# adaLN block on one core: weight-search counts by matmul, row maxima split before the transpose, and two moved products

## What is computed

```python
mod = (silu(c) @ wmod).reshape(8, 6, 1, 128)      # sa, ca, ga, sb, cb, gb
h = layernorm(x) * (1 + ca) + sa
x = x + ga * attention(h)                         # 16 heads of 8 dims, ALiBi bias, causal softmax
h = layernorm(x) * (1 + cb) + sb
x = x + gb * ffn(h)

def perturb(w):                                   # for W1, W2, b1, b2
    a = abs(w); s = sort(a.ravel()); k = int(n * 0.1 / 2)
    tier = where(a >= s[n - k], -1, where(a <= s[k - 1], 1, 0))
    return w + 0.8 * w * tier

def ffn(x):
    probs = softmax((layernorm(x) * gamma + beta) @ Wr + br)
    # expert 0 has the clean weights; experts 1 to 7 share the perturbed ones
    return sum_e probs[e] * (gelu(x @ W1[e] + b1[e]) @ W2[e] + b2[e])
```

## Time and profile before

| | |
|---|---|
| Time, median of 3 runs | 303.92 us (300.79 to 307.02) |
| Profiled execution: its own time | 301.41 us |
| Profiled execution: span, first to last instruction | 299.6 us |
| Mean granted PE clock | 0.901 |
| Busy: PE, DVE, ACT, POOL | 222.9, 213.6, 150.9, 135.8 us |
| Instructions | 5332 |

### The profile page before, as it was taken

The page is one execution under the profiler, slowest core; times in us unless marked ns, Lnnn a source line. Parts: engine busy times, 40 slices in busy tenths (PEclk is TensorE's granted clock), DMA queues, the critical chain, the costliest instruction groups (busy, mean ns, idle before and its releaser), DMA issues.

```text
span 299.6 us, 5332 instructions
## 1 busy us (share of the span) xinstructions
PE 222.9 (74%) x1799; PEld 150.0 (50%) x1799; DVE 213.6 (71%) x681; ACT 150.9 (50%) x337; POOL 135.8 (45%) x220
## 2 busy tenths in 40 slices
PE   2750575719886888877868488785983999999994
PEld 2340453517564666555546255453351467676674
DVE  2663499926998987989989359989586378626275
ACT  2322134326887757976786357763541743434430
POOL 8430089923855616536354024344635644443240
PEclk9999997556999979999999559997796699999999
DMA  7845556350250530433506200000000000101011
GB/s 218 178 94 139 150 141 244 86 144 0 73 142 21 150 82 23 128 85 82 150 0 170 63 1 2 3 2 2 2 1 2 0 1 2 35 1 37 0 35 35
DMA packets 17551, 20.42 MB, mean 68 GB/s; under 512 B 1446, under 2 KB 15413, under 8 KB 16317
## 3 DMA queue, kind: packets, MB, share of 16 engines
q1 hardware_dynamic: 14964, 18.98, 23.7%
q10 hardware_dynamic: 2048, 0.98, 1.2%
q0 software_dynamic: 512, 0.13, 0.3%
HBM read 14.70 MB, written 5.26 MB: 67 GB/s over the span
## 4 chain that ended last, share of the span: by engine, by line
PE 41%; DVE 25%; DMA 15%; POOL 10%; issue 6%; ACT 2%; SPq 0%; ACTq 0%; DVEq 0%; POOLq 0%
PE bank L746 10%; PE bank L728 10%; DMA Qs<-nmT 8%; DVE msk L939 7%; DVE nmax L970 5%; POOL hid L387 4%; PE bank L653 3%; DMA Ks<-parts 3%; DMA parts<-part 3%; PE bank L632 2%; PE bank L808 2%; PE bank L610 2%; DVE nmax L966 2%; PE bank L627 1%; POOL PT L400 1%
## 5 line engine op out<-in xcount | busy, mean ns | idle before, releaser
L400 POOL TENSOR_SCALAR_AFFINE_SELECT PT<-PT 128x256 f32<-128x256 f32 (+1 forms) x96 | 47.6, 500 | 80.1 <-ACT PT L453 77.4
L453 ACT ACTIVATE PT<-bank 128x512 f32<-128x512 f32 x96 | 53.5, 586 | 14.8 <-PE bank L627 13.7
L970 DVE TENSOR_REDUCE nmax<-bank 128x2 f32<-128x512 f32 x64 | 43.7, 683 | 20.7 <-PE bank L610 20.5
L365 POOL TENSOR_TENSOR ex<-eul,lg 128x32 f32<-128x32 f32 x4 | 21.7, 5428 | 27.8 <-DVE lg L1030 27.8
L606 PE MATMUL bank<-mask 128*128 128x256 bf16 x64 | 19.8, 309 | 12.0 <-DVE nmax L970 11.5
L610 PE MATMUL bank<-Ks,Qs 78*128 78x256 bf16 x128 | 28.6, 309 | 0.0
L966 DVE TENSOR_REDUCE nmax<-bank 128x4 f32<-128x512 f32 x32 | 21.7, 677 | 9.6 <-PE bank L603 9.6
L632 PE MATMUL bank<-Qs,Ks 80*128 80x256 bf16 x128 | 26.8, 293 | 0.6 <-ACT PT L453 0.5
L653 PE MATMUL bank<-PT,Vx 128*32 128x256 f32 x256 | 22.3, 422 | 5.4 <-POOL PT L400 5.2
L460 ACT ACTIVATE msk<-w1a,cand 128x512 bf16<-128x512 f32 x31 | 22.2, 715 | 6.7 <-DVE cand L933 3.9
L939 DVE TENSOR_SCALAR_CACHE_REDUCE msk<-w1a,cand 128x512 bf16<-128x512 f32 x31 | 23.1, 746 | 1.1
(11 more groups left out here) (181 smaller groups left out, 520.7 us busy)
## 6 DMA issues: line engine op xcount, KB each, us to landing
Qs<-parts SPq DMA_DIRECT2D x8, 576.0 KB
Ks<-parts SPq DMA_DIRECT2D x8, 576.0 KB
parts<-part SPq DMA_DIRECT2D x8, 384.0 KB, 2.9
rows_bc<-rows_out SPq DMA_DIRECT2D x4, 512.0 KB, 6.6
parts<-part SPq DMA_DIRECT2D x8, 128.0 KB, 3.6
out<-ob SPq DMA_DIRECT2D x3, 256.0 KB, 2.3
x_all<-in_x ACTq DMA_DIRECT2D x5, 128.0 KB, 8.5
w_sb<-in_w SPq DMA_DIRECT2D x2, 256.0 KB, 5.2
```

The lines of the kernel that those rows point to most:

```text
L400: gp.affine_select(out=v, in_=v, compare_op=ALU.is_ge, fill=0.0, base=0, pattern=[[0, v.shape[1]], [1, P]], channel_multiplier=-1).then_in ...
L453: act.activation(PT[:, e % 2, j], psE[u % 2][:, :], ACT.Exp).then_inc(q["exp_done"], 1)
L970: ve.tensor_reduce(nmax[:, b % 2, 1, h:h + 2], bank.rearrange("p (h k) -> p h k", h=2), axis=AX.X, op=ALU.max, negate=True).then_inc(q["ma ...
```

## The change

It does seven things.

- **Counts.** DVE's compares no longer accumulate; they write 0/1 masks. PE adds them with eight matmuls of one column each (counts), DVE copies the two sums to acc (count_copy), and total adds over partitions as before. counts stands right behind s_unit(t, 0), ahead of both e_units.
- **ACT's order.** exp_unit 0 and 1 stand ahead of the two sign passes, which are apart now; the U copy and exp_unit 2 stand behind them.
- **PE's order.** s_unit 1 ahead of pv, total behind pv, then s_unit 2, e_unit 2, ut, and OT and Y at the end of the step, in psX, the bank that the search uses (claim_x makes the next user wait for the last reader).
- **Maxima.** They are split by query in SBUF by DVE (split_maxima), and transposed as bf16 high and low parts in one product; ACT copies both at once.
- **Attention's front.** It begins one step earlier (t = -10), and ACT and DVE take up its products a step after PE makes them.
- **Fixed rows.** The constant rows of Qs and Ks come a rotation at a time, one with each stack; b1, b2 and x of batches 3 to 7 are loaded behind the first stack, and the magnitudes of W1 and W2 are taken later.
- **b2.** Its sizes, masks and perturbation move from steps -3 and -2 to steps 0 and 1; b1's rank masks start two steps later.

The core of the diff (`psO`, `psU` and `psX` are PSUM banks 4, 5 and 7):

```diff
 # SP
+            def fixed_rows(r):
+                sp.dma_start(Qs[R_PROD:R_S, r].rearrange("r h t -> r (h t)"), q_const).then_inc(const_in[r], 16)
+                sp.dma_start(Ks[R_PROD:R_E, r].rearrange("r h t -> r (h t)"), k_const).then_inc(const_in[r], 16)
-            sp.dma_start(Qs[R_PROD:R_S], rot(q_const)).then_inc(q["const_in"], 16)
-            sp.dma_start(Ks[R_PROD:R_E], rot(k_const)).then_inc(q["const_in"], 16)
                     stack(b)
+                    if b + 1 < ROTS:
+                        fixed_rows(b + 1)
+                    if b == 0:
...
+                        for k in range(3, B):
+                            sp.dma_start(x_all[:, k], x[k].rearrange("(i p) d -> p i d", p=P)).then_inc(x_in[k], 16)
 # ACT
             for t in range(T_FIRST, T_END):
-                if sel_bit(t) is not None:
-                    sign_counts(t)
...
                 exp_unit(t, 0)
+                exp_unit(t, 1)
+                if n is not None:
+                    sign_count(n, 2, w1a)
                 b = batch_at(t, AT_NMT)
...
+                    act.activation(nmT[:, b % 2, :], psO[0:3 * NH, 0:S], ACT.Copy).then_inc(q["nmr_done"], 1)
+                if n is not None:
+                    sign_count(n, 3, w2a)
...
+                b, g, e = lagged(t, E_LAG + 1)
+                if b is not None:
...
+                    act.activation(U[:, e % 2], psO[:, 0:S], ACT.Copy).then_inc(q["u_done"], 1)
+                exp_unit(t, 2)
 # PE
+            def counts(n):
+                claim_x((q["cnt_copied"], n + 1))
+                pe.wait_ge(q["m_dve"], n + 1)
+                for col in range(2):
+                    for j in range(NC):
+                        last = mm(psX[:, col:col + 1], msk[:, col, j * P:(j + 1) * P], ones_b[:, 0:1],
+                                  start=(j == 0), stop=(j == NC - 1), skip_group_check=True)
+                last.then_inc(q["cnt_done"], 1)
...
             for t in range(T_FIRST, T_END):
                 s_unit(t, 0)
+                counts(n)
...
                 e_unit(t, 0)
                 e_unit(t, 1)
+                s_unit(t, 1)
                 pv(t)
+                total(n)
+                s_unit(t, 2)
+                e_unit(t, 2)
+                ut(t)
                 b = batch_at(t, AT_OT)
...
                 b = batch_at(t, AT_Y)
                 if b is not None:
+                    claim_x((q["x2_done"], b + 1))
                     pe.wait_ge(q["wog_done"], b + 1)
...
-                    pe.wait_ge(q["a_done"], min(t - E_LAG - 1, B * G))
                     for i in range(NBLK):
+                        last = mm(psX[:, i * P:(i + 1) * P], AT[:, i * P:(i + 1) * P], woTg[:, b, :], start=True, stop=True)
 # DVE
-                    last = ve.tensor_scalar(msk[:, col], w[:, :], cand[:, col:col + 1].bitcast(F32), 0.0, op0=ALU.is_lt,
-                                            op1=ALU.add, accum_out=acc[:, col:col + 1])
+                    last = ve.tensor_scalar(msk[:, col], w[:, :], cand[:, col:col + 1].bitcast(F32), None, op0=ALU.is_lt)
+            def count_copy(n):
+                v.wait_ge(q["cnt_done"], n + 1)
...
+                ve.tensor_copy(acc[:, 0:2], psX[:, 0:2]).then_inc(q["cnt_copied"], 1)
+            def split_maxima(b):
...
+                ve.tensor_copy(nmHL[:, k, :, 0:NH], nmax[:, k]).then_inc(q["nm_self"], 1)
+                v.wait_ge(q["nm_self"], b + 1)
+                ve.tensor_tensor(nmHL[:, k, :, 2 * NH:3 * NH], nmax[:, k], nmHL[:, k, :, 0:NH], op=ALU.subtract).then_inc(q["nm_split"], 1)
```

More of the change, by code:

```diff
@@ L761, in _ @@
                 s_unit(t, 0)
+                counts(n)
+                b = batch_at(t, AT_NMT)
+                if b is not None:
+                    pe.wait_ge(q["nm_split"], b + 1)
+                    if b == 0:
+                        pe.wait_ge(q["dve_set"], SETS["all"])
+                    if t > E_LAG + 1:
+                        pe.wait_ge(q["u_done"], min(t - E_LAG - 1, B * G))
+                    for i in range(NBLK):
+                        last = mm(psO[0:3 * NH, i * P:(i + 1) * P], nmHL[:, b % 2, i, :], mask5[:, HG, :], start=True, stop=True)
+                    last.then_inc(q["nmT_done"], 1)
@@ L778, in _ @@
                     last.then_inc(q["y_done"], 1)
-                s_unit(t, 1)
-                e_unit(t, 2)
-                total(n)
-                b = batch_at(t, AT_NMT)
-                if b is not None:
-                    pe.wait_ge(q["max_done"], 3 * G * (b + 1))
-                    if b == 0:
-                        pe.wait_ge(q["dve_set"], SETS["all"])
-                    if t > E_LAG:
-                        pe.wait_ge(q["u_done"], min(t - E_LAG, B * G))
-                    for i in range(NBLK):
-                        last = tr(psO[0:NH, i * P:(i + 1) * P], nmax[:, b % 2, i, :], ident[:, :])
-                    last.then_inc(q["nmT_done"], 1)
@@ L1119, in _ @@
                 maxima(t, 0)
[L1120 to L1124 removed]
+                if n is not None:
+                    count_copy(n)
+                maxima(t, 1)
+                if n is not None:
+                    decide(n)
+                    next_cand(n)
+                if t == -1:
+                    first_cand()
+                if sel_bit(t + 1) is not None:
+                    dve_counts(t + 1)
+                    if n is not None:
+                        after_next(n)
                 b = batch_at(t, AT_SPLIT)
@@ L1165, in _ @@
                                      op=ALU.mult).then_inc(q["a_done"], 1)
+                b = batch_at(t, AT_Y)
+                if b is not None:
+                    v.wait_ge(q["y_done"], b + 1)
+                    ve.tensor_tensor(x_all[:, b], x_all[:, b], psX[:, 0:S].rearrange("p (i d) -> p i d", i=NBLK),
+                                     op=ALU.add).then_inc(q["x2_done"], 1)
                 if t in LN1_AT:
```

157 lines of the change are left out of this document (70 added, 87 removed).

## The result

The changed kernel takes 329.37 us (median of 4 executions, 327.95 to 329.72), the kernel before beside it 304.05 (300.79 to 307.02): ratio 1.0865, 95% interval 1.0808 to 1.0922. It is slower by 8.7%, 23 us above the forecast and 9 above its range. (The ratios in this document are formed from each kernel's undisturbed executions alone, those near its fastest, the medians from all, and the kernel before runs from 297 to 308 us; so ratios and medians can differ by one to three per cent.)

A forecast was written before the change was run, and what follows sets the result against it. Bounds: transfers first, then DVE, search rounds of 5.18 us (4.1 DVE's work), lastly PE in the FFN. Terms -4.2, -2.5, +8.5, +3, -1 gave +3.8 on 301.4: 305.2, plus 1, 306 us; range 291 to 320.

The forecast's parts named there:

- the search rounds with exponentials: Decision 6 to 30: a closed loop through four engines makes the 24 rounds 132.7 us against 124.2, +8.5 us.
- the clock: Search rounds: two more rounds with PE at 1.2 GHz, +3 us; as rival, half the rounds, 322 us, chance 0.18.
- The loop: Plain search round: decision, masks, counts, scores, exponentials, sign passes and total in series, 4.87 us.
- The long round: Search round from r = 3 to r = 0: maxima product and copy add 0.5 us, OT and V 0.45.
- The wait for Y's sum: Search, once a batch: next step's counts wait for DVE's sum of Y into x, 3.07 instead of 1.65, so 1.4 us.
- Start: Before the first scores: the parts' second write takes about 3.6 us instead of 7.8, -4.2 us.
- Steps 0 to 6: First scores to decision 6: cheaper masks, b2's work added on DVE, maxima rows landing just in time, -2.5 us.
- Steps 31 to 40: After the search rounds: OT and Y at other places, the FFN's front the same, -1 us.
- the loop would have to be 0.5 us a round shorter for a gain of 2%: Search rounds, rival: loop shorter than added and start gains more, 292 us, chance 0.25; this was the argument against it.
- The port: Rival, DVE's masks: POOL's work holds them up 0.3 us a round, +9, 314 us, chance 0.10.
- The transfer at step 26: Search rounds: the wait of about 6 us for maxima rows was assumed gone; if it stayed, some 5 us more.
- What would make me wrong: Search rounds: ACT's sign passes start before that round's masks are counted; rounds of 3.7 us, kernel under 285 us.

The follow-up runs named there:

- e1: Changed kernel with both of ACT's sign passes put back ahead of exponentials 0 and 1: 299.44 us against 303.22 for the kernel before, ratio 0.976.
- e10: Changed kernel with ACT's copy of the maxima product ahead of both sign passes and PE's product behind both blocks of scores for the exponentials: 317.52 us, ratio 1.0512.
- e3: Changed kernel with six useless matmuls per step, in steps 6 to 30, ahead of total's wait for the sign passes: 322.07 us, ratio 1.0692.
- e7: e1 with PE's product of the maxima moved behind e_unit(t, 1): 290.48 us against 304.54 for the kernel before, ratio 0.9762.
- e8: e7 with total also put ahead of pv on PE: 288.80 us, ratio 0.9686 to the kernel before.
- e5: Changed kernel with DVE's accumulating compares back, no count matmuls or count copy, exponentials still first: 320.86 us against 304.54 for the kernel before, ratio 1.0796.
- e11: Kernel before with only the first two exponentials put ahead of the sign passes on ACT: 310.34 us against 301.60, ratio 1.031.

## Why the prediction was wrong

The mechanism was right and its size was not. The step that failed is **the search rounds with exponentials: +8.5 us**, together with **the clock: +3 us**: they measured +29.4. The forecast of the 24 rounds was 135.7 us, and they took 153.6. Within it two terms were mis-sized, the half microsecond for the maxima's product and copy, and the clock's.

- **The loop.** I added 4.87 us for a plain round; at 2.4 GHz it took 5.00, with every link within 0.2 of where I had put it. r = 1 to 2 was forecast at 5.49 (4.87 and QK's 0.6) and took 5.48, r = 0 to 1 at 6.27 (4.87 and 1.4) and took 6.30. e1 shows that the loop is the cause: opened at ACT, it gives 30 us back.
- **The long round.** I put 0.5 us on r = 0's product and copy of the maxima, and with the 0.45 of OT and V 5.8 for the round from r = 3 to r = 0; it took 6.83 (at a clock of 0.94) to 8.38, mean 7.80. I had costed the copy as a piece between two sign passes, and not the product that waits for DVE's split in front of the scores, nor that PV, and with it the total, stands behind a copy which waits for a whole sign pass. e10, which repairs both, gives 12 us back, a part of it by a better clock.
- **The wait for Y's sum, 1.4 us a batch**, came out for the reason that I had given. In the changed kernel's two rounds of 6.30 us the chain goes through A and x_all to the counts, which start 3.3 us behind the total's start where I had 3.07; in e10 it is 3.1, with PE waiting 0.9 to 1.1 us. Where the clock was lower (the round from 183.20, at 0.80, PE busy for 4.97 of 6.43 us) PE came to the counts later than the sum did, so the table of waits shows only 0.3 us for it.
- **The clock, +3 us.** It was a rival at 0.18 (322 us, if half of the rounds ran at 1.2 GHz). Six batches of rounds at the highest clock seen would take 142 us, so the rounds at a lower clock cost the profiled execution about 12 us; the fill of e3 took 6 of them back, and more isn't shown. So the term was two to four times mine, and below the rival's 19. My price of such a round (6.5 us) was near for a plain one (round 18 to 19, at a clock of 0.50 throughout, took 6.15). What I had argued against the rival, that no single wait is as long as those ahead of the dips before, was true and no help: PE's longest pause in the rounds was 1.68 us, against 6.4 and 4.2 before, and the clock fell nine times.
- **Start: -4.2** measured -3.4. The write lands in 2.79 us; but it starts 1.0 us later, at the end of a chain that begins with w_o's load, which takes 6.47 us where it took 4.24. **Steps 0 to 6: -2.5** came out as +0.5 (36.65 us from the first scores to decision 6, 36.19 before): the maxima rows, 5.32 us, were still not in time, and landed only 1.0 us earlier behind the first scores, not 4.4. The 1.9 us that the decision should come later behind them measured 1.4; by the links of my own loop it would have been 0.9. Together -2.9 where I had -6.7. **Steps 31 to 40: -1** measured +1.9. All three lie within their bounds. The remark that the loop would have to be 0.5 us a round shorter for a gain of 2% was off too: 8 us over 24 rounds is 0.34.
- **The port** wasn't it. The masks measured 0.486 and 0.481 us on the median, against the 0.476 that I took:

```profile
L960 DVE TENSOR_SCALAR msk<-w1a,cand x31: 485/486/732, 23.4 to 215.0; 128x512 bf16<-128x512 f32 x31
L960 DVE TENSOR_SCALAR msk<-w2a,cand x31: 473/481/915, 23.8 to 215.4; 128x512 bf16<-128x512 f32 x31
```

  Four of the 62 took 0.73 to 0.92 us, all before 68 us, and one 0.56.
- **The transfer at step 26** that held up the kernel before is not in the chain of the changed kernel's rounds, as I had assumed: PE waited for maxima rows only once, 1.4 us at step 6, against four times and 13.6 us before. Its transfers of maxima rows took 1.9 us on the median and 5.3 at most.
- **What would make me wrong** I had put at the other side: sign passes ahead of the masks' counting, under 285 us. With just that (e1) the kernel takes 299: the long round stays at 6.9 us, and a round with DVE's sum for the split (resid, 0.60) in its chain takes 4.25 us; only the rounds without batch-wise work take 3.70. e7 and e8 remove the first.

In sum: 29.4 against 8.5 + 3. Of the excess of 18 about 9 is there at the highest clock (6 the long round, 1 the plain rounds, 2 the first four rounds, which I had put lower), and the other 9 is rounds at a lower clock beyond my 3. That split is worked out from the shortest rounds of the profiled execution (6.30 + 5.48 + 5.00 + 6.83 = 23.6 a batch, six of them 142; the first and the last of these at clocks of 0.89 and 0.94). The experiments confirm that each part is there and not the split: e10's 12 us hold some of the clock's, and e3 and e10 were not run together.

## What to carry to other kernels

Before a wait is moved to another engine, write out the closed chain from decision to decision through every in-order queue; where a reduction that decides something shares an engine with throughput work, it goes first. Once such a chain is closed a round lasts its whole length (5.00 us here, with DVE busy for 4.07), and it also draws each later batch-wise piece (a copy, a product that waits for a split) into its length: those once-a-batch pieces need the same accounting as the plain round, each with what it waits for and what stands behind it.

A part that relieves the busiest engine gains nothing while the chain goes through others: the count matmuls took 0.4 us a round off DVE, and in the changed kernel they cost 8.5 us. The wait of the deciding instruction (0.3 us in the kernel before, 16 in e1, 38 in e5, 44 in the changed kernel) is a first sign of a closed chain, though a rough one: e11 lost 9 us with 5.2 of it.

## What the runs showed of the hardware

- With useless matmuls added the kernel was 7 us faster (e3), and PE's granted clock in the profiled rounds was 0.94 in place of 0.77. In the closed loop PE was busy for 3.73 of 5.00 us in a plain round, in pieces, with no pause over 1.68 us, and its clock fell to 1.2 GHz nine times; in e1 and e8 it stood at 0.92 and 0.94 in the same stretch.
- The mean clock of an execution is a poor guide to its time: 0.778 and 0.908 lie 1.7 us apart in the changed kernel.
- The parts' write of 128 KB took 2.79 us with one rotation's constant rows ahead of it and 7.79 with four and other loads.
- The 8 KB transfer of maxima rows at step 6 took 5.32 us in the changed kernel and 8.64 in e1, where the medians of such transfers are 1.9 and 2.4.
